# A wait for landing behind each two scatters of token rows in a fused attention and expert kernel

## The chip, the cores and the metric

The kernel runs on one core of one Trainium2 chip. The metric is the device time of one execution in microseconds (us), taken without the profiler; the median of three runs is given. A profile is one further execution of the same program, recorded by the hardware profiler.

## The reference, cut to what matters

```python
x = x + attention(rigid_transform(x, shift, angle))      # 2 x 1024 tokens of 256, 16 heads, causal
f = reaction_diffusion(x)                                # second differences along both axes
logits = f @ W_router + b_router                         # 8 experts
top_vals, top_idx = top_k(logits, 2)
w = softmax over the two chosen experts
for e in range(8):
    h = relu(f @ W1[e] + b1[e])                          # 256 -> 1024
    y = h @ W2[e] + b2[e]                                # 1024 -> 256
    out = out + y * w[:, e]                              # w is 0 where e was not chosen
x = x + out
```

Each of the 2048 tokens needs two experts only, so the kernel sorts tokens by expert and computes 39 tiles of 128 sorted rows.

## The kernel before, in words

One core does everything, with one instruction stream for each engine and semaphores between them. The order of the work is written out by hand.

**Stages.** First the image is sheared and interpolated, then attention runs in eight groups (four of heads for each of the two batches b = 0 and b = 1). Beside the last groups of b = 1 the router of b = 0 is computed. Then come the expert tiles. Nine of them (EARLY_TILES, tiles 0 to 8) hold rows of b = 0 alone, and the rest of b = 1 (its output projection, its reaction step, its router) is computed between them in a hand-written list (EARLY). The other 30 tiles are a loop.

**Scatters.** When the router of a batch has set each token's place (DVE, lines 1940 to 1966), GpSimd (POOL) writes the token rows to a sorted table `pairs_x` in HBM: function scatter (line 1010), one indirect DMA for 128 rows of 1032 bytes at line 1016, for each of the batch's 8 blocks and each of the two choices k. That is 16 scatters for a batch. All count on one semaphore, `scattered`, 16 for each.
- Batch 0: 16 scatters in a row, while attention of b = 1 ends on TensorE (PE) and ScalarE (ACT).
- Batch 1: between the expert tiles. Blocks go two by two (4 scatters); behind the second two stands add_tile(2), behind the fourth two add_tile(3).

**An expert tile t.** SyncE (SP) loads its rows (line 733, x_tile, from `pairs_x`), its W1 (line 720) and its W2 (line 726), 1 MB each, three tiles deep. PE turns the rows (turn_x, line 1478), makes the first product (line 1487), turns the hidden rows (line 1494) and makes the second product (line 1503). DVE copies the hidden rows out (line 2050) and in y_out adds the bias and scales (lines 2066, 2070), which signals `y_ready`. ACT applies the relu (line 1229). POOL adds the tile's result to HBM in add_tile (line 1020, an accumulating indirect DMA at line 1026).

**What ties them.** SP's row loads of tiles 0 to 2 wait for all 16 scatters of batch 0 (line 748), and four weight loads stand behind them in SP's queue. The row load of tile 9 waits for all 32. PE runs in order, so everything behind turn_x(0) waits for the rows of tile 0. y_out(t) waits until add_tile(t - 3) has landed, since there are three y_tile buffers: `dve.wait_ge(y_stored, (t - (SLOTS - 1)) * 16)`. The second product of tile t waits until y_out(t - 1) has read the bank. add_tile(t) waits for y_out(t) and for add_tile(t - 1) to land. POOL runs in order too: add_tile(2) and (3) stand behind the scatters ahead of them.

pool_hold (line 771) is a wait of POOL followed by an increment of a semaphore that nothing waits for.

Of the kernel before, what the change touches and what calls it, by code (L numbers as in the profile page):

```python
# [179 lines left out]
def build(nc, x, shift, angle, zx, zy, zr, wq, bq, wk, bk, wv, bv, wo, bo, wr, br, w1, b1, w2, b2, consts, out):  # L180
    ctx = ExitStack()
    with ctx:
# [3 lines left out]
        def sem(name):  # L186
            return ctx.enter_context(nc.semaphore(name))
# [256 lines left out]
        scattered = sem("scattered")  # L444
# [55 lines left out]
        def attention_plan():  # L500
# [19 lines left out]
            for n in range(2 * NG):  # L520
# [16 lines left out]
                if n == NG + 3:  # L537
# [16 lines left out]
                 ("first", 8, 0), ("second", 7, 0), ("h", 8, 0), ("second", 8, 0)]  # L554
        LIST_BEHIND, LAST_BEHIND = ("second", 3), ("first", 6)
        assert sum(k for _, _, k in EARLY) == len(LAST_PLAN)
        BEHIND, at_ = {}, 0
        for what_, t_, k_ in EARLY:
# [212 lines left out]
        def pool_hold(semaphore, value):  # L771


            nc.gpsimd.wait_ge(semaphore, value)
            nc.gpsimd.sem_inc(pool_held, 1)
# [61 lines left out]
        def _(pool):  # L837
# [172 lines left out]
            def scatter(b, blocks):  # L1010

                pool.wait_ge(slots_ready, b + 1)
                pool.wait_ge(weighed, b + 1)
                for i in blocks:
                    for k in range(2):
                        g_.indirect_dma_start(pairs_x.rearrange("r d -> (r d)").unsqueeze(0),  # L1016
                                              bass.IndirectOffsetOnAxis(ap=x_index[:, k, i:i + 1], axis=1),
                                              du_rows[:, i, 2 - 2 * k:ROW - 2 * k], None).then_inc(scattered, 16)

            def add_tile(t):  # L1020
                pool_hold(y_ready, t + 2)
                if t:
                    pool_hold(y_stored, 16 * t)
                if t == FIRST_LAST:
                    pool_hold(copied, 16)
                g_.indirect_dma_start(results if t < FIRST_LAST else out.rearrange("b s d -> (b s) d"),  # L1026
                                      bass.IndirectOffsetOnAxis(ap=home[:, t:t + 1], axis=0), y_tile[t % SLOTS],
                                      None, compute_op=ALU.add).then_inc(y_stored, 16)
# [4 lines left out]
            for n in range(NG + 2, 2 * NG):  # L1033
                group_of_v(n)
            pool.wait_ge(pairs_cleared, 16 * (NG + 1))
            scatter(0, range(SB))
            sideways(1)
            pool.wait_ge(base_stored, 16)
            for t in range(2):
                add_tile(t)  # L1040
            for k in range(SB // 2):
                scatter(1, range(SB + 2 * k, SB + 2 * k + 2))
                if k % 2:
                    add_tile(2 + k // 2)
# [496 lines left out]
        def _(dve):  # L1541
# [367 lines left out]
            def choose(b):  # L1909

                own = slice(b * SB, (b + 1) * SB)
                iota = const("experts").unsqueeze(1).broadcast_to([P, SB, E])
                lg_, cand_, idx_ = lg[:, own], cand[:, own], route[:, 6, own]

                def wide(a):
                    return a.unsqueeze(2).broadcast_to([P, SB, E])

                for turn, hot in enumerate((hot_1[:, own], hot_2[:, own])):
                    m = route[:, 2 + turn, own]
                    steps.do(v.reduce_max(m, lg_, AX_X))  # L1920
                    tt(cand_, lg_, wide(m), ALU.is_equal)
                    stt(cand_, iota, float(-E), cand_, ALU.add, ALU.mult)
                    steps.do(v.tensor_reduce(idx_, cand_, AX_X, ALU.min))
                    ts(idx_, idx_, float(E), ALU.add)
                    tt(hot, iota, wide(idx_), ALU.is_equal)
                    if turn == 0:
                        stt(lg_, hot, -3.0e38, lg_, ALU.mult, ALU.add)
                tt(both[:, own], hot_1[:, own], hot_2[:, own], ALU.add)
                dve.sem_inc(chosen_ready, 1)
                gap, _, m1, m2 = (route[:, i, own] for i in range(4))  # L1930
                tt(gap, m2, m1, ALU.subtract)
                dve.sem_inc(gap_ready, 1)
# [200 lines left out]
```

## Time and profile before

| what | value |
|---|---|
| median of 3 runs without the profiler | 964.36 us (960.53 to 966.77) |
| span of the profiled execution, first to last instruction | 990.0 us |
| time of the profiled execution itself | the page gives its span alone |
| PE busy | 732.5 us, 74% of the span |
| DVE, ACT, POOL busy | 52%, 36%, 31% |
| chain that ended last, largest shares | PE 55%, DVE 17%, DMA 10% |
| the same chain, "another core or an unknown queue" | 3% |

The median is 25.6 us below the profiled span. POOL's rows for an indirect DMA show the time in which the engine writes descriptors; the transfer itself comes later and is seen in the rows of queue q0 (software_dynamic). q1 (hardware_dynamic) carries the loads that SP issues. A wait marked "remote" and the chain's "another core or an unknown queue" mean that the profile shows no instruction whose end lies near the end of the wait.

### The profile page before, as it was taken

The page shows a single profiled execution, that of the slowest core. Times are in us where ns is not written, and L with a number is a line of the kernel's source. Part 1 is how long each engine was busy: PE and PEld are TensorE (multiplying, and loading weights), DVE is VectorE, ACT ScalarE, POOL GpSimd, SP SyncE. Part 2 cuts the span into 40 slices and gives each one's busy share as a digit, 9 for nine tenths or more (in the row PEclk, how much of TensorE's full clock was granted, in tenths as well). Part 3 has the DMA queues.
Part 4 walks back from the last instruction along what each step waited for, and adds up shares of the span by engine and source line. Part 5 has one row for each costly group of instructions (what it writes and reads, how often), then busy time and mean ns, then how long its engine had stood idle before and what let it go on. Part 6 is the DMA issues. An engine that isn't in the chain of part 4 may idle for free.

```text
span 990.0 us, 13623 instructions
## 1 busy us (share of the span) xinstructions
PE 732.5 (74%) x4035; PEld 437.9 (44%) x4035; DVE 515.9 (52%) x1052; ACT 360.4 (36%) x912; POOL 310.5 (31%) x292
## 2 busy tenths in 40 slices
PE   0440122835878889888999949997779999999993
PEld 0430111421333434433455413774557777666663
DVE  6446555777557664767777732654323333333331
ACT  0222333361566635363654535210212222222220
POOL 1114454876789623001100061107211111122121
PEclk9875555867899999999999979998899999999997
DMA  6998887896753017979310043957669999899961
GB/s 212 311 272 312 293 305 248 307 292 218 225 180 140 3 65 245 334 232 353 111 45 1 2 129 119 302 187 223 202 214 309 295 293 302 287 374 297 296 183 16
DMA packets 136206, 216.13 MB, mean 218 GB/s; under 512 B 10357, under 2 KB 102058, under 8 KB 135978
## 3 DMA queue, kind: packets, MB, share of 16 engines
q1 hardware_dynamic: 114808, 150.78, 46.5%
q0 software_dynamic: 16784, 61.51, 19.8%
q10 hardware_dynamic: 4546, 3.08, 1.1%
q8 instruction: 25, 0.41, 0.2%
q14 instruction: 43, 0.35, 0.1%
HBM read 160.87 MB, written 56.37 MB: 219 GB/s over the span
## 4 chain that ended last, share of the span: by engine, by line
PE 55%; DVE 17%; DMA 10%; issue 6%; ACT 4%; another core or an unknown queue 3%; POOL 2%; SPq 1%; ACTq 0%; POOLq 0%; DVEq 0%
PE psum L1503 13%; PE psum L1487 13%; DVE arena L1734 7%; PE psum L1428 6%; PE psum L1257 5%; PE psum L1442 5%; PE psum L1494 3%; DMA arena<-table,tap_col 3%; DMA arena<-qk_rows 2%; DMA table<-arena 2%; ACT arena L1180 2%; PE psum L1391 1%; POOL arena L881 1%; PE psum L1270 1%
## 5 line engine op out<-in xcount | busy, mean ns | idle before, releaser
L1180 ACT ACTIVATE arena<-psum 128x512 f32<-128x512 f32 (+3 forms) x384 | 171.2, 492 | 151.8 <-PE psum L1447 95.5
L1734 DVE TENSOR_REDUCE arena<-psum 128x2 f32<-128x1024 f32 (+2 forms) x192 | 176.2, 955 | 68.7 <-PE psum L1263 47.2
L1229 ACT ACTIVATE arena<-psum,b_cols 128x128 f32<-128x128 f32 x312 | 84.7, 382 | 269.9 <-PE psum L1494 248.0
L1503 PE MATMUL psum<-arena 128*128 128x256 f32 x624 | 147.2, 391 | 12.7 <-ACT arena L1229 12.7
L1487 PE MATMUL psum<-arena 128*128 128x512 f32 x312 | 142.8, 601 | 1.9 <-issue 1.8
L1442 PE MATMUL psum<-arena 99*128 99x512 bf16 (+3 forms) x384 | 115.9, 340 | 28.8 <-ACT arena L1180 23.0
L1503 PEld LDWEIGHTS psum<-arena 128*128 128x128 f32 x624 | 119.8, 197 | 30.1 <-issue 14.2
L1257 PE MATMUL psum<-arena 96*128 96x512 bf16 (+3 forms) x384 | 107.8, 347 | 33.6 <-DMA arena<-qk_rows 17.5
L2050 DVE COPY arena<-psum 128x1024 f32<-128x1024 f32 x39 | 47.8, 1225 | 93.7 <-PE psum L1487 92.4
L1428 PE MATMUL psum<-arena 128*32 128x512 f32 (+3 forms) x768 | 86.1, 521 | 0.5 <-ACT arena L1180 0.5
L1026 POOL DMA_INDIRECT results<-arena,home x23 | 36.4, 1581 | 156.0 <-DVE arena L2070 105.9
L1487 PEld LDWEIGHTS psum<-arena 128*128 128x128 f32 x312 | 57.1, 193 | 59.9 <-issue 59.9
L2066 DVE TENSOR_TENSOR arena<-psum,arena 128x256 f32<-128x256 f32 x39 | 16.6, 425 | 126.9 <-PE psum L1503 93.6
L1257 PEld LDWEIGHTS psum<-arena 96*128 96x128 bf16 x384 | 35.3, 102 | 104.4 <-DVE arena L1734 52.1
L1442 PEld LDWEIGHTS psum<-arena 99*128 99x128 bf16 x384 | 37.9, 100 | 80.1 <-ACT arena L1180 50.6
L1307 PE MATMUL psum<-cst,arena 128*128 128x128 f32 x16 | 5.5, 447 | 89.5 <-DVE arena L1773 89.5
L1298 PE MATMUL psum<-cst,arena 128*128 128x128 f32 (+1 forms) x180 | 33.9, 372 | 49.8 <-DMA arena<-padded,band_col 47.6
L1026 POOL DMA_INDIRECT result<-arena,home x16 | 24.8, 1552 | 103.6 <-DMA result<-arena,home 61.9
L1447 PE MATMUL psum<-mask_kq,ident_b 128*128 128x128 bf16 x256 | 54.9, 224 | 0.0
L1263 PE MATMUL psum<-mask_qk,ident_b 128*128 128x128 bf16 x256 | 54.1, 230 | 0.0
L1298 PEld LDWEIGHTS psum<-cst,arena 128*128 128x128 f32 (+1 forms) x180 | 30.9, 190 | 52.2 <-issue 36.1
L1016 POOL DMA_INDIRECT pairs_x<-warped_words,x_index x32 | 31.0, 969 | 66.8 <-DVEq L1944 57.7
(215 smaller groups left out, 985.2 us busy)
## 6 DMA issues: line engine op xcount, KB each, us to landing
arena<-L_ffn_W SPq DMA_DIRECT2D x78, 1024.0 KB, 5.4
pairs_x<-zeros SPq DMA_DIRECT2D x4, 4160.0 KB, 25.8
arena<-qk_rows SPq DMA_DIRECT2D x16, 768.0 KB, 7.2
table<-arena SPq DMA_DIRECT2D x20, 384.0 KB
qk_rows<-arena SPq DMA_DIRECT2D x16, 384.0 KB, 6.2
arena<-pairs_x SPq DMA_DIRECT2D x39, 130.0 KB, 4.6
qk_rows<-arena SPq DMA_DIRECT2D x16, 256.0 KB, 6.3
padded<-arena SPq DMA_DIRECT2D x2, 1328.0 KB
```

The lines of the kernel that those rows point to most:

```text
L1026: g_.indirect_dma_start(results if t < FIRST_LAST else out.rearrange("b s d -> (b s) d"), bass.IndirectOffsetOnAxis(ap=home[:, t:t + 1], a ...
L1180: nc.scalar.activation(probs[at % 2][h][:, q0:512], banks[turn % SCORE_BANKS][:, q0:512], ACT.Exp, scale=DH ** -0.5).then_inc(exp_done, 1)
L1229: ins = nc.scalar.activation(hidden_t[:, f], banks[3 + f // 4][:, (f % 4) * P:(f % 4 + 1) * P], ACT.Relu, bias=b1_cols[:, bass.ds(e, 1), f])
L1257: ins = t_.matmul(bank[:, 0:keys], stacks[0:KROWS, bass.ds(g, 1), 0, head, qb * P:(qb + 1) * P].squeeze(1).squeeze(1), stacks[0:KROWS, bas ...
L1263: ins = t_.matmul(bank[:, at_:at_ + P], ident_b[:], mask_qk[:], start=False, stop=True)
L1298: ins = t_.transpose(banks[g][0:w, r * P:(r + 1) * P], band[u][:, at_:at_ + w], ident)
L1428: ins = t_.matmul(banks[OUT_BANK][32 * h:32 * h + 32, q0:512], v_group[:, n % 2, kt, h], probs[at % 2][h][:, q0:512], start=first, stop=last)
L1442: ins = t_.matmul(bank[:, q0 - half * 512:512], stacks[0:KROWS + 3, g, 1, h, kt * P:(kt + 1) * P], stacks[0:KROWS + 3, g, 0, h, q0:(half + ...
L1447: ins = t_.matmul(bank[:, at_:at_ + P], ident_b[:], mask_kq[:], start=False, stop=True)
L1487: ins = t_.matmul(banks[half], x_t[:, c], w1_slot[u][:, c, half * 512:(half + 1) * 512], start=c == 0, stop=c == DC - 1)
L1503: ins = t_.matmul(banks[5][:, 0:D], hidden_t[:, f], w2_slot[u][:, f], start=f == 0, stop=f == FC - 1)
L1734: return v.reduce_max(part[:, 2 * pair:2 * pair + 2, qb], psum[:, first:first + 2, 0:keys], AX_X)
```

## The change

Behind the two scatters of each block, POOL waits until all scatters so far have landed.

```diff
@@ -1016,6 +1016,7 @@
                         g_.indirect_dma_start(pairs_x.rearrange("r d -> (r d)").unsqueeze(0),
                                               bass.IndirectOffsetOnAxis(ap=x_index[:, k, i:i + 1], axis=1),
                                               du_rows[:, i, 2 - 2 * k:ROW - 2 * k], None).then_inc(scattered, 16)
+                    pool_hold(scattered, 16 * 2 * (i + 1))
 
             def add_tile(t):
                 pool_hold(y_ready, t + 2)
```

POOL's instructions for batch 0, before: the first scatter waits for the router's places, and the other 15 follow it.

```order
L1016 DMA pairs_x<-warped_words,x_index 1x4293120 [waits weighed,slots_ready,pairs_cleared]
L1016 DMA pairs_x<-warped_words,x_index 1x4293120 x15
L831 TENSOR_TENSOR arena<-x 128x2x254 [waits reacted,x1_ready]
L832 TENSOR_SCALAR arena<-x 128x2
L833 TENSOR_SCALAR arena<-x 128x2
```

The same place on POOL in the changed kernel (its first pairs; the pattern repeats up to the eighth).

```order
L1016 DMA pairs_x<-warped_words,x_index 1x4293120 [waits weighed,slots_ready,pairs_cleared]
L1016 DMA pairs_x<-warped_words,x_index 1x4293120
L1016 DMA pairs_x<-warped_words,x_index 1x4293120 [waits scattered]
L1016 DMA pairs_x<-warped_words,x_index 1x4293120
L1016 DMA pairs_x<-warped_words,x_index 1x4293120 [waits scattered]
L1016 DMA pairs_x<-warped_words,x_index 1x4293120
```

Nothing changes places; every second scatter now carries a wait for `scattered`.

POOL's instructions for batch 1, before: the blocks of four scatters, with add_tile(2) and add_tile(3) (L1026) between and behind them.

```order
L1016 DMA pairs_x<-warped_words,x_index 1x4293120 [waits weighed,slots_ready]
L1016 DMA pairs_x<-warped_words,x_index 1x4293120 x3
L1016 DMA pairs_x<-warped_words,x_index 1x4293120 [waits weighed,slots_ready]
L1016 DMA pairs_x<-warped_words,x_index 1x4293120 x3
L1026 DMA results<-arena,home 2176x256 [waits y_ready,y_stored]
```

The same place on POOL in the changed kernel, where the line of add_tile's DMA is L1027.

```order
L1016 DMA pairs_x<-warped_words,x_index 1x4293120 [waits weighed,slots_ready]
L1016 DMA pairs_x<-warped_words,x_index 1x4293120
L1016 DMA pairs_x<-warped_words,x_index 1x4293120 [waits scattered]
L1016 DMA pairs_x<-warped_words,x_index 1x4293120
L1016 DMA pairs_x<-warped_words,x_index 1x4293120 [waits scattered,weighed,slots_ready]
L1016 DMA pairs_x<-warped_words,x_index 1x4293120
L1016 DMA pairs_x<-warped_words,x_index 1x4293120 [waits scattered]
L1016 DMA pairs_x<-warped_words,x_index 1x4293120
L1027 DMA results<-arena,home 2176x256 [waits scattered,y_ready,y_stored]
```

Four such waits now stand ahead of add_tile(2), the last on its own instruction, and four more ahead of add_tile(3). The other engines' instructions are the same in both kernels.

## Rows read from the trace of the kernel before

**Rows 1.** Chain that ended last, 570 to 600 us: start us, us, what.
```profile
576.94 4.68 another core or an unknown queue
...
584.67 8.28 another core or an unknown queue
```
**Rows 2.** The same view, 670 to 725 us.
```profile
674.78 21.24 another core or an unknown queue
```
**Rows 3.** Timeline, 674 to 712 us: start us, us, engine, line, operation [idle before <- releaser].
```profile
675.34 3.62 PE L1503 MATMUL psum<-arena 128*128 128x256 f32 x16
...
684.48 1.97 PE L1494 MATMUL psum<-cst,arena 128*128 128x128 f32 x8 [5.52 <-issue]
686.24 5.76 PE L1487 MATMUL psum<-arena 128*128 128x512 f32 x8
694.59 0.42 DVE L2066 TENSOR_TENSOR arena<-psum,arena 128x256 f32<-128x256 f32 x1 [9.64 <-remote]
696.68 2.17 ACT L1229 ACTIVATE arena<-psum,b_cols 128x128 f32<-128x128 f32 x8 [21.89 <-remote]
698.95 6.30 PE L1503 MATMUL psum<-arena 128*128 128x256 f32 x16 [6.73 <-ACT arena L1229]
705.09 1.04 PE L1494 MATMUL psum<-cst,arena 128*128 128x128 f32 x8
705.96 3.60 PE L1487 MATMUL psum<-arena 128*128 128x512 f32 x8
```
**Rows 4.** Waits of SP's queue: total us, times, longest us.
```profile
SPq L715 <- remote: 16.5, 1, 16.5
```
**Rows 5.** Timeline of POOL, 560 to 800 us.
```profile
572.91 1.06 POOL L1016 DMA_INDIRECT pairs_x<-warped_words,x_index  x1 [42.33 <-DVEq L1944]
574.27 0.99 POOL L1016 DMA_INDIRECT pairs_x<-warped_words,x_index  x1 [0.30 <-issue]
...
592.10 0.96 POOL L1016 DMA_INDIRECT pairs_x<-warped_words,x_index  x1 [0.30 <-issue]
653.23 1.61 POOL L1026 DMA_INDIRECT results<-arena,home  x1 [13.31 <-DVE arena L2070]
670.20 0.99 POOL L1016 DMA_INDIRECT pairs_x<-warped_words,x_index  x1 [15.36 <-DVEq L1944]
692.41 1.61 POOL L1026 DMA_INDIRECT results<-arena,home  x1 [0.30 <-issue]
697.48 1.59 POOL L1026 DMA_INDIRECT results<-arena,home  x1 [3.46 <-issue]
716.67 1.55 POOL L1026 DMA_INDIRECT results<-arena,home  x1 [7.41 <-DMA results<-arena,home]
723.97 1.55 POOL L1026 DMA_INDIRECT results<-arena,home  x1 [5.76 <-issue]
```
**Rows 6.** DMA queues, 594 to 595 us: packets, MB, share of 16 engines.
```profile
q0 software_dynamic: 15, 0.00, 0.8%
```
**Rows 7.** Timelines: SP's row load, DVE's scaling, PE at tile 0 and tile 7.
```profile
595.74 2.40 SPq L733 DMA_DIRECT2D arena<-pairs_x  x3
612.38 0.44 PE L1478 MATMUL psum<-cst,arena 128*128 128x128 f32 x2
651.98 0.36 DVE L2070 TENSOR_SCALAR arena<-arena,weight 128x256 f32<-128x256 f32 x1
717.38 3.62 PE L1503 MATMUL psum<-arena 128*128 128x256 f32 x16
```
**Rows 8.** DMA issues, 560 to 610 us: KB each, us to landing.
```profile
arena<-pairs_x SPq DMA_DIRECT2D x3, 130.0 KB, 2.0
```
**Rows 9.** Busy time by stretch: A:B us, PE, PEld, DVE, ACT, POOL, PEclk, DMA share, GB/s.
```profile
684.00:690.00 6.00, 5.52 (x13) 3.43 (x14) 0.95 (x4) 0.00 (x0) 4.48 (x6) 0.50 0.38 128
```
**Rows 10.** DMA queues, 581 to 584 us.
```profile
q1 hardware_dynamic: 179, 0.73, 86.4%
```

## The prediction

> **What bounds the kernel now.** I read the chain that ended last first, because PE is busy 74% of the span and the question is what the rest is. In the two stretches where POOL scatters, the chain has its only large pieces of "another core or an unknown queue": 4.68 and 8.28 us in batch 0 [rows 1] and 21.24 us in batch 1 [rows 2]. Next the timeline, to see who waits there. In batch 1 DVE's L2066 waits 9.64 us and ACT's L1229 21.89 us for something "remote" [rows 3], and SP's queue waits 16.5 us in the same way [rows 4]. By the code, DVE and SP wait for the second product of tile 4 and ACT for the turned hidden rows of tile 5. Their PE rows end at 675.34 + 3.62 = 678.96 and at 684.48 + 1.97 = 686.45 [rows 3], some 16 and 10 us before the waits end. So PE had done the work, by its rows, and its signals reached three engines late, while POOL was issuing scatters. I call this the held signals. In batch 0 it is ACT that waits, also for PE.
>
> What they cost the profiled execution, from the chain: batch 0, 4.68 + 8.28 = 13.0 us, all in attention's last group. Batch 1: PE finished first product and turned rows at 686.24 + 5.76 + 0.2 = 692.2 and could start the second product of tile 5 only at 698.95, 6.7 us; that product then took 6.30 us instead of 3.62 (PE had stood still), another 2.7. Together 22.4 us. The rest of the 21.24 us is covered by PE's own work and by DVE's list of tiles, which PE waits for (5.52 us) either way.
>
> The decisive number is another: the runs without the profiler take 964.36 us, 25.6 us less than the profiled span of 990.0. If the held signals belong to the profiled execution only, the sum closes to 3.2 us (990.0 - 22.4 = 967.6). I know of no other 22 us that a recorder could add to a kernel whose PE rows have the same durations tile after tile. So I take it as likelier that the timed runs have few or none of these stalls, and that the change has little to win there.
> The Trainium skill (NOTIFIC, the notification-queue block, section 7.1) says that the block which writes the profiler's records can push back on the engines that produce them, though it was never seen to overflow. That would be such a cause; the trace cannot tell it from a real hold on the signals.
>
> **The change part by part.** It adds 16 waits on POOL and moves nothing. Each pair of scatters now costs its own round trip. Within a pair: second scatter starts 574.27 - 572.91 = 1.3 us after the first [rows 5]. Landing: the last scatter of batch 0 starts at 592.10, and the last packets of q0, empty ones, fall in 594 to 595 [rows 5, 6], so 2.0 us after its start. Restart of POOL after a wait: DVE's L2070 ends at 651.98 + 0.36 = 652.34 and the add starts at 653.23, 0.9 us [rows 5, 7]. A pair's period is 1.3 + 2.0 + 0.9 = 4.2 us, against 2.6 before. From below: the restart costs no more than the 0.30 us between scatters, 3.6. From above: SP's row load, released by the last scatter, is issued at 595.74, 3.64 us after that scatter's start [rows 5, 7]; 1.3 + 3.6 = 4.9.
>
> Term C, rows of tile 0 come late. Batch 0 starts at 572.9 as before. The eighth pair starts at 572.9 + 7 x 4.2 = 602.3, plus 0.5 for the pair in flight while SP's first W1 load has the engines: from 581 to 584 there is no q0 packet, though POOL issued three scatters around it [rows 10]. It lands at 602.8 + 3.3 = 606.1, not 594.1. SP needs 1.6 us from landing to issue (594.1 to 595.74) and the rows 2.0 more [rows 7, 8]: 609.7. PE reaches turn_x(0) at 612.38 in the profile [rows 7] and at 612.4 - 13.0 = 599.4 without held signals. There it waits, in order, with everything behind it: +10.3 us. With a period of 3.6 it is +6, with 4.9 +15. In the profiled execution alone the wait would have hidden behind the stall (609.7 is before 612.4): this is where a gain of 13 us turns into one of 2.7.
> The Trainium skill (DMA: Bandwidth & Descriptors, "Queues, rings and completion order") says that each DMA engine goes round between its queues packet by packet. By that rule the pair in flight would share with the W1 load and the 0.5 us would be 0, and the waits of batch 1 would be close to the unloaded 4.2. The trace does not agree in 581 to 584, where q1 has 179 packets and q0 none.
>
> Term D, the clock. PE stands still some 10 us ahead of turn_x(0). After such a pause the granted clock is 0.50, the 1.2 GHz level, for about 6 us [rows 9], and the rows show what it costs: L1494 1.97 instead of 1.04 and L1487 5.76 instead of 3.60 [rows 3]; 3.1 us. Bounds 0 and 5.
>
> Term E, the adds behind the scatters of batch 1. Queued behind POOL's waits stand add_tile(2) and (3), and y_out(6) waits for add_tile(3) to land, second product 7 for y_out(6). With a period p from 670.2 [rows 5]: four pairs, add_tile(2) with 1.9 us of POOL, four pairs, add_tile(3), its landing 4.2 us later (692.41 to 697.48 less the restart), y_out: second product 7 can start at 670.2 + 8p + 7.0. Unloaded (p = 4.2) that is 710.8. But the weight loads run beside it, and adds that wait for their landing come 723.97 - 716.67 = 7.3 us apart there, against 5.1 at 692 to 697 when SP was stuck [rows 5]; 2 us more each. So p lies between 4.2 and 6.2; when PE stalls, the loads stop and p falls back, and I take 5.2: 718.8. Without held signals that product would start at 717.38 - 9.4 = 708.0 [rows 7]. +10.8 us, bounds 3 and 19. add_tile(4) follows 5 us behind and holds nothing more, and the row load of tile 9 is needed later.
>
> Sum of costs: 10.3 + 3.1 + 10.8 = 24.2 us. On the profiled execution: 990.0 - 22.4 + 24.2 = 991.8 us, so its span hardly moves. On the timed runs, without anything to win: 964.4 + 24.2 = 988.6 us. Every term's row comes from the one profiled execution; the median is taken as the base because I hold its stalls for absent.
>
> **The rivals.**
> Rival 1, the held signals are real and in the timed runs too, and pairs dissolve them. For it: three engines truly waited in the trace, and only beside scatters. Against it: then 25.6 us between span and median have no source. Time: 964.4 - 22.4 + 24.2 = 966.2, within 1%.
> Rival 2, the same, and the round trips are cheap, so that it ends faster. One mechanism: PE's signals flow during the scatters, and landing is quick enough not to take the place of the stall. It decides at costs under 12.8 us (22.4 - 9.6). With the low ends, C 6, D 1, E 3: 964.4 - 12.4 = 952.0. For it: add_tile(2) and (3) would only just be late at p = 3.6 to 4.2. Against it: the loads beside batch 1, and PE's start on tile 0, which is bound to the last landing in every case.
> Rival 3, the change doesn't do what it says: POOL's waits cost nothing that anyone waits for, 964 us. It would take landings that keep up with issue; the 2.0 us of rows 5 and 6 speak against it.
> Rival 4, held signals stay with two scatters in flight as with sixteen: PE's signals were still prompt behind the first four scatters of batch 0 (the first hole starts at 576.94, 4 us after the first scatter), so pairs with pauses should be too short for it. If they stay, the cost terms stand alone and the time is the forecast's.
>
> **How the numbers follow.** Forecast (with rival 4) 0.60, own range 974 to 1004 (the terms' low ends 6 + 0 + 3 and high ends 15 + 5 + 19). Rival 1 0.25, 957 to 981. Rival 2 0.08. Rival 3 0.07. About 1%, 9.6 us, is what a measurement of this kernel can tell from no change. Faster by more: rival 2 and a corner of rival 1, 0.10. Slower by more: nearly all of the forecast and a part of rival 1, 0.64. Within: 0.26. The range 957 to 1001 leaves out rival 2 and the forecast's upper tail.
>
> **What would show each step.** In the changed kernel's profile: scatters in twos, 4.2 us from pair to pair in batch 0; no "unknown queue" piece in the chain over 2 us beside them; the row load of tile 0 issued near 607.7 and PE's L1478 near 609.7, with the clock at 0.50 behind it; an L2066 of tile 6 that waits for the landing of an add near 718; a span near 992. I am wrong if the profile's span falls by 15 us or more (the costs were too high), and wrong about the base if the span stays near 990 while the median stays near 964: then the timed runs had the stalls.

## The result, and the profile after

The changed kernel takes 1008.83 us (median of 4 runs, 1006.52 to 1013.25), the kernel before 965.57 us (median of 4 runs, 960.53 to 967.66). The ratio is 1.0453, 95% interval 1.0411 to 1.0495: slower by 43.3 us. The forecast was 988.6 with a range to 1001; the direction was right and the size was not. The profiled execution took 1006.52 us by itself, with a span of 1004.3, so what the recorder sees and what the clock outside sees are 2.2 us apart. A few executions ran in a slower state (1102.42 us in one of the last kernel of the table below), which the ratios leave out and the medians do not; over the others alone the medians of "before, small loads" and "before, four adds moved" are 964.1 and 964.7.

The chain of the changed kernel in batch 0 (start us, us, what) answers to [rows 1].

```profile
577.26 5.91 DMA pairs_x<-warped_words,x_index
583.21 0.77 issue
583.97 0.97 POOL pairs_x L1016
585.25 2.43 DMA pairs_x<-warped_words,x_index
...
588.49 0.97 POOL pairs_x L1016
...
607.93 2.75 DMA pairs_x<-warped_words,x_index
611.44 2.12 DMA arena<-pairs_x
614.30 3.71 PE psum L1381 x8
...
628.29 3.63 PE psum L1488 x8
```

No piece of "unknown queue" is left. In its place the chain runs through every pair: 1.27 us between its two scatters, 2.43 to 2.75 us landing, 0.77 us until POOL starts the next, some 4.5 in all. One pair took 5.91 us to land. The same view in batch 1 answers to [rows 2].

```profile
676.66 6.92 DMA pairs_x<-warped_words,x_index
...
685.66 6.47 DMA pairs_x<-warped_words,x_index
...
694.26 2.43 DMA pairs_x<-warped_words,x_index
...
698.77 6.29 DMA pairs_x<-warped_words,x_index
706.03 1.61 POOL results L1027
...
722.94 2.58 DMA pairs_x<-warped_words,x_index
726.49 3.78 DMA results<-arena,home
732.07 6.58 PE psum L1504 x16
```

Three of the first four pairs needed 6.3 to 6.9 us to land (the third 2.43), and the pairs behind add_tile(2) 2.4 to 2.6. The second product of tile 7 (PE L1504, L1503 before) starts at 732.07, behind the landing of add_tile(3). The timeline shows SP's loads, and who waits for the late pieces.

```profile
577.00 0.42 SPq L720 DMA_DIRECT2D arena<-L_ffn_W  x1
611.44 2.58 SPq L733 DMA_DIRECT2D arena<-pairs_x  x3
613.61 0.69 PE L1479 MATMUL psum<-cst,arena 128*128 128x128 f32 x2 [18.59 <-DMA arena<-pairs_x]
675.37 0.99 POOL L1016 DMA_INDIRECT pairs_x<-warped_words,x_index  x1 [15.34 <-DVEq L1945]
676.36 0.38 SPq L726 DMA_DIRECT2D arena<-L_ffn_W  x1
685.25 12.48 SPq L726 DMA_DIRECT2D arena<-L_ffn_W  x2
698.61 0.38 SPq L720 DMA_DIRECT2D arena<-L_ffn_W  x1
710.65 0.42 DVE L2067 TENSOR_TENSOR arena<-psum,arena 128x256 f32<-128x256 f32 x1 [13.20 <-DMA results<-arena,home]
711.61 6.58 PE L1504 MATMUL psum<-arena 128*128 128x256 f32 x16 [10.37 <-DVE arena L2071]
726.25 1.47 SPq L733 DMA_DIRECT2D arena<-pairs_x  x2
731.11 0.42 DVE L2067 TENSOR_TENSOR arena<-psum,arena 128x256 f32<-128x256 f32 x1 [17.99 <-DMA results<-arena,home]
732.07 6.58 PE L1504 MATMUL psum<-arena 128*128 128x256 f32 x16 [9.57 <-DVE arena L2071]
```

These answer to [rows 3, 5, 7]: nothing waits for "remote" any more. Each slow pair has a 1 MB weight load issued beside it (577.00, 676.36, 685.25, and for the fourth pair of batch 1 the second load of the row at 685.25, issued near 697.4, and the one at 698.61). PE waits 18.59 us for the rows of tile 0, and 10.37 and 9.57 us for products 6 and 7.

### The profile page after: what moved, and what is told of

The parts are those of the page before. It is cut to its first block, busy times and chain, and to the rows that moved or that the text cites. A ratio compares the mean times of both kernels' runs of the same rounds, so it can differ in the third digit from the quotient of the medians.

```text
span 1004.3 us, 13639 instructions
## 1 busy us (share of the span) xinstructions
PE 732.9 (73%) x4035; PEld 440.9 (44%) x4035; DVE 515.1 (51%) x1052; ACT 359.8 (36%) x912; POOL 312.2 (31%) x292
## 4 chain that ended last, share of the span: by engine, by line
PE 49%; DVE 18%; DMA 16%; issue 7%; POOL 4%; ACT 3%; SPq 1%; POOLq 0%; DVEq 0%; ACTq 0%
PE psum L1504 12%; PE psum L1488 12%; DVE arena L1735 7%; DMA pairs_x<-warped_words,x_index 6%; PE psum L1429 5%; PE psum L1258 5%; PE psum L1443 4%; DMA arena<-table,tap_col 3%; PE psum L1495 3%; DMA table<-arena 3%; DMA arena<-qk_rows 2%; POOL arena L881 2%; POOL pairs_x L1016 2%; PE psum L1392 1%; PE psum L1271 1%
## 5 line engine op out<-in xcount | busy, mean ns | idle before, releaser
L1504 PE MATMUL psum<-arena 128*128 128x256 f32 x624 | 147.2, 391 | 25.9 <-DVE arena L2071 19.9
L1504 PEld LDWEIGHTS psum<-arena 128*128 128x128 f32 x624 | 119.7, 197 | 43.5 <-issue 27.7
L1443 PE MATMUL psum<-arena 99*128 99x512 bf16 (+3 forms) x384 | 113.8, 334 | 15.7 <-ACT arena L1181 9.9
L2051 DVE COPY arena<-psum 128x1024 f32<-128x1024 f32 x39 | 47.8, 1225 | 94.1 <-PE psum L1488 93.8
L1429 PE MATMUL psum<-arena 128*32 128x512 f32 (+3 forms) x768 | 83.0, 504 | 0.5 <-ACT arena L1181 0.5
L1027 POOL DMA_INDIRECT results<-arena,home x23 | 36.4, 1581 | 146.6 <-DVE arena L2071 57.6
L1299 PE MATMUL psum<-cst,arena 128*128 128x128 f32 (+1 forms) x180 | 36.2, 390 | 49.5 <-DMA arena<-padded,band_col 47.6
L1443 PEld LDWEIGHTS psum<-arena 99*128 99x128 bf16 x384 | 37.5, 99 | 64.3 <-ACT arena L1181 37.8
L1027 POOL DMA_INDIRECT result<-arena,home x16 | 25.0, 1560 | 101.5 <-DMA result<-arena,home 57.3
L1299 PEld LDWEIGHTS psum<-cst,arena 128*128 128x128 f32 (+1 forms) x180 | 33.0, 200 | 51.8 <-issue 36.2
## 6 DMA issues: line engine op xcount, KB each, us to landing
pairs_x<-zeros SPq DMA_DIRECT2D x4, 4160.0 KB, 25.6
arena<-qk_rows SPq DMA_DIRECT2D x16, 768.0 KB, 11.4
```

Of the source, the lines that this page charges most:

```text
L1299: ins = t_.transpose(banks[g][0:w, r * P:(r + 1) * P], band[u][:, at_:at_ + w], ident)
L1429: ins = t_.matmul(banks[OUT_BANK][32 * h:32 * h + 32, q0:512], v_group[:, n % 2, kt, h], probs[at % 2][h][:, q0:512], start=first, stop=last)
L1443: ins = t_.matmul(bank[:, q0 - half * 512:512], stacks[0:KROWS + 3, g, 1, h, kt * P:(kt + 1) * P], stacks[0:KROWS + 3, g, 0, h, q0:(half + ...
L1504: ins = t_.matmul(banks[5][:, 0:D], hidden_t[:, f], w2_slot[u][:, f], start=f == 0, stop=f == FC - 1)
```

## The experiments

Four distances, all read from the timelines, put the runs side by side: from the first scatter of batch 0 to SP's load of the first rows (a), from the first scatter of batch 0 to that of batch 1 (b), from there to SP's load of tile 9's rows, which waits for all 32 scatters (c), and from there to the end of the span (d). The profiled kernel ahead of the prediction had 22.8, 97.3, 38.3 and 281.5. Where the text below gives a run's distance from the kernel before, it is from the 966.2 us of the first row.

| kernel | median us | ratio to before, 95% interval | a | b | c | d |
|---|---|---|---|---|---|---|
| before, again | 966.2 | 0.999 (0.995 to 1.002) | 22.6 | 85.9 | 25.0 | 281.2 |
| the change | 1008.8 | 1.045 (1.041 to 1.050) | 40.4 | 104.3 | 50.9 | 278.1 |
| batch 0 alone | 983.8 | 1.019 (1.013 to 1.026) | 40.6 | 105.2 | 25.0 | 283.2 |
| batch 1 alone | 991.9 | 1.026 (1.021 to 1.032) | 22.7 | 87.7 | 51.8 | 281.3 |
| one pair behind | 978.4 | 1.011 (1.006 to 1.017) | 26.8 | 90.7 | 36.9 | 278.0 |
| behind each four | 989.1 | 1.024 (1.020 to 1.028) | 29.3 | 93.7 | 39.3 | 282.4 |
| W1 behind the rows | 1010.7 | 1.046 (1.041 to 1.050) | 37.7 | 105.0 | 50.3 | 282.4 |
| small loads | 1000.3 | 1.038 (1.032 to 1.043) | 41.1 | 105.6 | 41.3 | 278.1 |
| before, small loads | 964.8 | 0.998 (0.994 to 1.002) | 22.7 | 85.9 | 24.8 | 280.2 |
| two adds moved | 1006.9 | 1.042 (1.038 to 1.046) | 40.8 | 106.3 | 51.5 | 276.1 |
| before, two adds moved | 965.4 | 0.999 (0.997 to 1.001) | 22.6 | 84.3 | 25.5 | 279.5 |
| four adds moved | 997.5 | 1.035 (1.029 to 1.041) | 40.6 | 104.4 | 54.5 | 263.5 |
| before, four adds moved | 966.3 | 1.002 (0.999 to 1.005) | 22.5 | 84.2 | 34.1 | 269.5 |

### The kernel before, profiled again

No edit.

> The kernel before, unchanged, for a profile of a usual execution. If the held signals belong to the rare execution that was profiled first: a span near 963 us, no 'unknown queue' piece above 2 us in the chain beside the scatters, PE at tile 0's rows (L1478) about 26.5 us behind the first scatter of batch 0 and the second product of tile 7 about 38 us behind the first scatter of batch 1. If they are in every execution: a span near 990 us and those pieces again.

Ten runs, 959.43 to 970.65, one of them profiled: span 966.1, its own time 968.07. The chain has no piece of unknown queue, and the scatters run one into the next until SP loads the rows.

```profile
590.67 0.97 POOL pairs_x L1016
591.94 0.97 POOL pairs_x L1016
593.22 2.63 DMA pairs_x<-warped_words,x_index
596.61 2.08 DMA arena<-pairs_x
...
599.17 1.92 PE psum L1380 x8
...
602.14 4.67 PE psum L1487 x8
...
611.12 5.33 PE psum L1487 x8
```

And from its timeline:

```profile
598.74 0.44 PE L1478 MATMUL psum<-cst,arena 128*128 128x128 f32 x2 [0.76 <-DMA arena<-pairs_x]
659.92 0.99 POOL L1016 DMA_INDIRECT pairs_x<-warped_words,x_index  x1 [15.36 <-DVEq L1944]
693.98 3.62 PE L1503 MATMUL psum<-arena 128*128 128x256 f32 x16
```

Two things follow. The held signals belong to the one execution profiled first: b and c were 11.4 and 13.3 us longer in it, 24.7 together, where the prediction had put them at 22.4. And PE reached the first rows 598.74 - 574.01 = 24.7 us behind the first scatter, after a wait of 0.76 us, so the rows of tile 0 were already just on the path: no slack at all. Both distances that the prediction had worked out by subtraction are shorter: 24.7 us where 26.5 was expected, and 693.98 - 659.92 = 34.1 us to the second product of tile 7 where 38 was expected.

### The hold in one batch alone

```diff
-                    pool_hold(scattered, 16 * 2 * (i + 1))
+                    if b == 0:
+                        pool_hold(scattered, 16 * 2 * (i + 1))
```

> The waits in batch 0 alone. Theory (round trips in series; each batch has its own path to the end): terms C and D as the changed kernel's trace has them, 16 + 4 = 20 us, so 985 us. Rival (the batches share one path, so that a shift ahead of the expert tiles is taken up by slack later, and batch 1 makes the whole cost): within 5 us of the kernel before, 970 us or less. PE at tile 0's rows 42 to 43 us behind the first scatter in either case.

The other run has `if b == 1:` in that place.

> The waits in batch 1 alone. Theory: term E as the changed kernel's trace has it, 19 to 23 us, so 985 to 989 us, and together with the run for batch 0 the 43 us of the change. Rival (shared path): 1000 us or more. y_out of tiles 5 and 6 wait for an add to land, over 10 us each.

Measured: 983.84 us with batch 0's holds and 991.87 with batch 1's, 17.6 and 25.6 us above 966.2. The first is within 2 us of the 985 expected, the second just above the 985 to 989 expected, and both rivals (970 or less, 1000 or more) fall. The sum, 43.2, is the change's 43.3: the halves add up and neither covers for the other. In the table batch 0's holds lengthen a and b and leave c; batch 1's lengthen c alone. Both are well above the terms of the prediction (13.4 for C and D, 10.8 for E).

### Waiting for the pair before the last

```diff
-                    pool_hold(scattered, 16 * 2 * (i + 1))
+                    if i:
+                        pool_hold(scattered[(i - 1) % 2], 32 * ((i - 1) // 2 + 1))
```

with two semaphores, counted in turn by block.

> As many waits as the change, but each for the pair before the last (two semaphores, one for even and one for odd blocks), so that two pairs can be in flight. Theory (the cost is the round trip in series): without load the pair before has landed when the wait is reached (2.6 us of issue against 2.4 of landing), the period falls to 2.6 to 2.9 us in batch 0, and beside weight loads some waiting stays: 966 to 976 us. Rival (each wait of POOL costs by itself, by its restart, whatever it waits for): a period near 3.5 to 4.5 us in batch 0 and 985 to 1005 us.

Measured 978.44 us, just above the 966 to 976 expected, 12 above before and 30 below the change: most of the cost is POOL standing through each landing, and it goes when the wait looks one pair back. The timeline of POOL shows the part that stays.

```profile
581.08 0.96 POOL L1018 DMA_INDIRECT pairs_x<-warped_words,x_index  x1 [0.30 <-DMA pairs_x<-warped_words,x_index]
...
588.61 0.97 POOL L1018 DMA_INDIRECT pairs_x<-warped_words,x_index  x1 [4.03 <-DMA pairs_x<-warped_words,x_index]
...
675.18 0.96 POOL L1018 DMA_INDIRECT pairs_x<-warped_words,x_index  x1 [5.09 <-DMA pairs_x<-warped_words,x_index]
```

Between most pairs POOL waits no longer than the 0.30 us it always has. It stands 4.03 us at 588.61, behind a W1 load issued at 580.99, and in batch 1 5.09 at 675.18 and again 4.77 and 3.76 us at 684.71 and 695.16. That was more than expected, and it pointed to the weight loads.

### Holding behind each four scatters

```diff
-                    pool_hold(scattered, 16 * 2 * (i + 1))
+                    if i % 2:
+                        pool_hold(scattered, 16 * 2 * (i + 1))
```

> The change with the hold behind every second block only: GpSimd waits behind each four scatters, so eight holds instead of sixteen. Theory, each hold costs its own round trip (2.4 us landing and 0.8 until the next scatter starts, less the 1.3 us... of one scatter's spacing: 2.0 us of 4.5 in place of 2.5) and a hold that meets a weight load about 3.5 to 4.3 us more: batch 0 three restarts fewer costs 6 + 3.5 + 3 for the cold clock = 12 to 13 instead of 17.6; batch 1, with three of its four holds meeting a load, 10 to 15 instead of 25. Together 988 to 994. Rival, the cost is in meeting the loads and not in the number of waits: then batch 0 costs nearly what it did, and the time stays above 998. Rival, the cost goes by the number of waits alone: half of 43, 988 or less.

989.06 us, inside the first theory's interval, but only just above what "by the number of waits alone" gave, so the time does not tell these two apart. The distances do in part: in batch 0, where here no wait met a load (each ended 2.4 to 2.9 us behind the last scatter's start), a is 6.7 us above before (22.6 to 29.3), as three restarts at 2.0 say; c rose by 14.3, with two of its landings above 6 us.

### W1's load behind the row loads

```diff
-            load_w1(0)
             sp.wait_ge(scattered, 16 * NBLK)
             for t in range(SLOTS):
                 load_x(t)
+            load_w1(0)
```

> The change with the load of the first expert's W1 issued behind the first three row loads instead of among batch 0's scatters. Theory: a pair of scatters in flight gets little or nothing from the DMA engines while a weight load runs, so the second pair's 8.0 us (5.9 us landing) come from that load, and all pairs of batch 0 now take 4.5 us; the first rows are loaded 3.5 us earlier behind the first scatter (about 37 us instead of 40.4). In time: 3.5 us less at most, 1005.3, and nothing if W1, now loaded some 6 us ahead of the first product, lands too late. Rival: the long second pair belongs to the start of the scatters and not to the load; then it stays at 8 us, and the time at 1009 or above.

The second pair's landing is the first in this piece of chain, and the next bound is the second.

```profile
579.28 2.48 DMA pairs_x<-warped_words,x_index
...
614.06 5.65 DMA arena<-L_ffn_W
619.75 6.77 PE psum L1488 x8
```

With the load gone the pair lands in 2.48 us instead of 5.91 and all pairs of batch 0 take 4.5 to 5.0 us: the load, not the start of the scatters, held it. The rows are loaded 2.7 us earlier (a 37.7, where about 37 was expected). But the time did not fall, 1010.7 (1005.51 to 1014.52): W1 now lands at 619.7 and the first product starts at 619.75, 46.8 us behind the first scatter; in the change it started at 618.85, 47.8 behind. What is gained on the rows goes into W1 and a slower start of PE (its first product takes 6.77 us instead of 4.91). The expected 3.5 us were a ceiling, and the case "W1 too late" came.

### Small weight loads beside batch 1's scatters

```diff
-                sp.dma_start(w1_slot[t % SLOTS], w1[bass.ds(expert_of(t), 1)].squeeze(0)
-                             .rearrange("(c p) f -> p c f", p=P)).then_inc(w1_in[t % SLOTS], 16)
+                wide = P if t in (8, 9) else FC * P
+                sp.dma_start(w1_slot[t % SLOTS][:, :, 0:wide], w1[bass.ds(expert_of(t), 1)].squeeze(0)
+                             .rearrange("(c p) f -> p c f", p=P)[:, :, 0:wide]).then_inc(w1_in[t % SLOTS], 16)
```

and W2 likewise, cut to `[:, 0:1]` of its eight parts for t in (6, 7, 8). Both kernels of this section leave out the rest of these weights, so they measure time only.

> The change with five weight loads that fall among batch 1's scatters cut to an eighth (W2 of tiles 6, 7, 8 and W1 of tiles 8, 9: 128 KB instead of 1 MB each; the rest of those weights is left out, so the output of these tiles differs). Theory, a pair in flight gets nothing from the DMA engines while a 1 MB weight load runs: in the changed kernel four of batch 1's eight pairs take 6.3 to 7 us to land (periods 8.6 to 9.0) and each has such a load issued in it; with small loads all eight land in 2.4 to 2.8 us, and from the first scatter of batch 1 to SP's load of tile 9's rows it takes 37 to 41 us instead of 50.9. In time 995 to 999. Rival, the long landings come from the adds or from the place of the rows written, not from the loads: four pairs stay above 5 us and the time within 4 us of 1008.8.

And the control:

> The control of the run ahead of it: the kernel before, without holds, with the same five loads cut to an eighth. Its sixteen scatters run without a wait at 1.27 us each, so the loads cost them nothing; only adds and products that met a load can gain. Theory: 960 to 967, so that the change beside its small loads costs 30 to 34 us instead of 43. Rival, small loads help everything behind them alike: then this run gains as much as the other, and is at 955 or below.

DMA issues of batch 1 in the small-loads kernel, 675 to 717 us (count, KB each, median us from issue to landing):

```profile
arena<-L_ffn_W SPq DMA_DIRECT2D x5, 128.0 KB, 2.3
pairs_x<-warped_words,x_index POOLq DMA_INDIRECT x16, 2.6
```

The same in the run with batch 1's holds and whole loads, 657 to 690 us:

```profile
arena<-L_ffn_W SPq DMA_DIRECT2D x5, 1024.0 KB, 6.6
pairs_x<-warped_words,x_index POOLq DMA_INDIRECT x9, 4.2
```

With five loads cut to an eighth, c falls from 50.9 to 41.3, where 37 to 41 was expected, and no pair of batch 1 takes over 3.9 us to land. The time is 1000.33, 8.5 below the change (997.47 to 1003.30; 995 to 999 was expected, a narrow miss). The control is unmoved at 964.83, so the gain is the holds' own. Beside small loads the change costs 1000.3 - 964.8 = 35.5 us, a little above the 30 to 34 expected. (The expectation spoke of four slow pairs in batch 1; the profile shown above has three.) So about 8 of the 43 us are batch 1's pairs standing behind weight loads. The other 35 stay with no large load beside batch 1's scatters. That they are the round trips themselves is what the run one pair behind says, which gives 30 of the 43 back with all loads in place; batch 0's one pair behind W1 is among the 35, and freeing that gained nothing.

### Moving adds ahead of batch 1's scatters

```diff
-            for t in range(2):
+            for t in range(3):
                 add_tile(t)
             for k in range(SB // 2):
                 scatter(1, range(SB + 2 * k, SB + 2 * k + 2))
-                if k % 2:
-                    add_tile(2 + k // 2)
+                if k == 0:
+                    add_tile(3)
```

> The change with two adds moved on GpSimd: the add of tile 2 goes ahead of batch 1's scatters, the add of tile 3 behind the first four of them (in the change they stand behind the first eight and behind all sixteen). Theory A, the cost of the second batch comes through the buffers of the products: in the changed kernel's profile second product 6 waits for the add of tile 2 (issued 706.03) and product 7 for the add of tile 3 (726.49). With both early, products 6 and 7 wait for nothing, and the next that can wait is product 8, for the add of tile 4, which still stands behind all sixteen scatters (near 722, landing near 726). Product 8 stood at 742.48 and would stand near 728 to 730: 12 to 15 us less, 993 to 997. If adds 2 and 3 were the whole of the second batch's cost it would fall to what the hold in batch 0 alone costs, 984. Rival B, the length of the scatters itself sets the time, through the rows of tile 9 that SP loads behind them (726.25): then within 4 us of the change, 1005 to 1009.

1006.89 us. By the time alone rival B has it. The profile says otherwise.

```profile
702.62 3.62 PE L1504 MATMUL psum<-arena 128*128 128x256 f32 x16
710.38 3.62 PE L1504 MATMUL psum<-arena 128*128 128x256 f32 x16
736.64 6.56 PE L1504 MATMUL psum<-arena 128*128 128x256 f32 x16 [21.77 <-DVE arena L2071]
...
746.86 6.57 PE L1488 MATMUL psum<-arena 128*128 128x512 f32 x8 [3.44 <-issue]
```

Products 6 and 7 wait for nothing, as theory A had it, and the whole wait reappears in one piece, 21.77 us, ahead of product 8, which needs add_tile(4) from behind all sixteen scatters. A chain of adds with three buffers was unblocked at two links and stood at the third. Then DVE's y_out for tile 8 waits 8.87 us for add_tile(5), which lands late beside the loads that SP had held back. DVE's copy of tile 9's turned rows stands behind that y_out (it starts at 746.36), and so PE's first product of tile 9 starts at 746.86.

With four adds moved (tile 2 ahead, tiles 3, 4 and 5 behind four, eight and twelve scatters):

```diff
-                if k == 0:
-                    add_tile(3)
-            for t in range(4, EARLY_TILES):
+                if k < 3:
+                    add_tile(3 + k)
+            for t in range(6, EARLY_TILES):
```

> The change with four adds among or ahead of batch 1's scatters: tile 2 ahead of them, tiles 3, 4 and 5 behind four, eight and twelve. With two moved adds (1006.9) the wait went to product 8, which stood 21.8 us for the add of tile 4 behind all sixteen scatters. Theory A, only the adds' place couples the scatters to the products: product 8 then runs near 720, some 16 us earlier, the next thing behind the scatters is SP's load of tile 9's rows near 735, which turn and first product of tile 9 use; 993 to 999. Rival B, the end of batch 1's scatters sets the time whatever is moved on GpSimd (in all eight traces so far the span ends 276 to 283 us behind SP's load of tile 9's rows): 1004 to 1010.

997.47 us (991.60 to 1001.12), inside theory A's interval; rival B falls. The span now ends 263.5 us behind SP's load of tile 9's rows where all kernels up to this one had 276 to 283. By itself that says little: the load also comes 3.6 us later (c 54.5), since adds now stand among the scatters, and in the kernel before with the same moves, below, d falls by 11.7 us with the time unchanged. What counts is c and d together, which fall by 11. PE's timeline:

```profile
705.19 3.62 PE L1504 MATMUL psum<-arena 128*128 128x256 f32 x16
712.62 5.38 PE L1504 MATMUL psum<-arena 128*128 128x256 f32 x16 [2.94 <-ACT arena L1230]
728.10 0.69 PE L1479 MATMUL psum<-cst,arena 128*128 128x128 f32 x2 [10.10 <-DMA arena<-pairs_x]
729.36 5.95 PE L1488 MATMUL psum<-arena 128*128 128x512 f32 x8 [0.56 <-issue]
```

Product 8 starts at 712.62 and does not wait for an add. The wait is now 10.10 us for the rows of tile 9, which SP may load only when all scatters have landed. So the adds carried some 11 us of batch 1's cost (1008.8 - 997.5), and behind them stood a second bound, the rows.

### The same moves without holds

Both moves in the kernel before, as candidates to beat it.

> The kernel before, without holds, with the same two adds moved: tile 2 ahead of batch 1's scatters, tile 3 behind the first four. If the adds behind sixteen unheld scatters already hold the products a little (in the profile of the kernel before run again, second product 5 comes 12.9 us behind product 4 where its neighbours take 8.2 to 8.5, and the add of tile 2 is issued 17 us after its product), 960 to 964 against 966.2. Rival: what delays product 5 is the batch's other work on TensorE and VectorE, and the adds cost nothing in the kernel before: 965 to 968. Slower than 970 only if batch 1's scatters, which start about 2 us later, set something: rows of tile 9 are loaded 684.9 and used behind 705, so this has some 20 us of slack.

> The kernel before, without holds, with the same four adds moved; the candidate to beat both. With two moved adds it stood at 965.4, and product 8 still waited 2.95 us for ScalarE and 1.8 to 2.9 us followed ahead of tile 9's first product. If these come from the adds of tiles 4 and 5, which land 6 to 7 us apart behind the scatters, 960 to 963. If adds behind sixteen scatters at 1.27 us have slack enough, 964 to 967. Above 968 only if the later end of the scatters (some 3 to 5 us) is late for tile 9's rows.

965.41 and 966.26 us, no difference from 966 in either. Behind sixteen scatters at 1.27 us apart the adds have slack enough. The 2.95 us that product 8 waits for ScalarE in the kernel before are still there in both, so they did not come from adds. With four adds moved the rows of tile 9 are loaded 9.1 us later (c 34.1) and no one waits for them. No version tried beats the kernel before.

## Why the prediction was right in direction and short in size

**The base was right.** "The timed runs have few or none of these stalls" holds: the second profile has none, its span is 2 us below its own time, and its 966.1 stands beside the 967.6 that the subtraction of 22.4 us gave. That was the step that turned a seeming gain into a loss. Rivals 1, 2 and 4 needed the held signals in the usual execution and fall with them; rival 3 falls by the 43 us. The reverse has to be said too: that the profile of the change shows no held signals proves nothing for pairs, since the kernel before shows none either in its usual execution.

**Term C, the rows of tile 0, failed in size: 10.3 us forecast, 17.8 measured.** PE's first turn_x stands 613.61 - 571.05 = 42.6 us behind the first scatter, 24.7 before. Three steps of the working were off. The period of an undisturbed pair was put at 4.2 us and is 4.54: the landing was read as 2.0 from packets (2.43 to 2.75 by the semaphore), the restart as 0.9 (0.77). With the first pair's 4.94 that is 2.4 us over six periods. The pair beside the W1 load was charged 0.5 us and takes 7.98 instead of 4.54: 3.3 more than charged. And PE without stalls was put at 26.5 us behind the first scatter, 1.8 too late. The third part shows a habit worth dropping: a stall was subtracted from one execution and the rest taken as exact, although removing a stall also removes what it had pushed back.

**Term D, the clock, 3.1 forecast, 0.6 measured.** From the first turn_x to batch 1's first scatter the change takes 675.37 - 613.61 = 61.76 us, the kernel before 659.92 - 598.74 = 61.18. The slow rows are there after the long pause (granted clock 0.50 from 613.6 to 618.0; L1381 3.71 where before had 1.92), but the kernel before has slow rows of its own a little later (0.51 from 601 to 604), in its first product (4.67, the change 4.91) and its second one (5.33, where the change has 3.63). The cost of a clock level was counted as if the other kernel had none.

**Term E, the adds behind the scatters, 10.8 forecast, 22.6 measured.** The mechanism was right: product 7 waits for add_tile(3), at 732.07, and the formula 8p + 7.0 gives 56.2 us behind the first scatter with the measured p against 56.7 read. The step that failed is the choice of p = 5.2. Measured, (726.49 - 675.37 - 1.92) / 8 = 6.15 us, nearly the upper bound of 6.2: three pairs take 8.5 to 9.0 and five 4.5 to 4.8, since a load in the way costs a pair some 4 us and not 2. That is 8 x 0.95 = 7.6 us. The reason given for 5.2, "when PE stalls, the loads stop and p falls back", is not what happened. The third pair is quick because SP issues no load from 685.7 to 697.4, and the kernel before profiled again has a like gap (670.2 to 682.4). From the fifth pair on it is SP itself that stands: its queue waits for all 32 scatters ahead of tile 9's rows, with every later load behind. SP's waits, 670 to 730 us (total us, times, longest us):

```profile
SPq L732 <- DMA pairs_x<-warped_words,x_index: 26.5, 1, 26.5
```

That tile 9's row load waits for all scatters was known; that it holds back the weight loads too was not drawn from it. Another 3.7 us of the difference in term E are the base of product 7, put 37.8 us behind the first scatter and found at 34.1 in the kernel before profiled again. "The row load of tile 9 is needed later" was true only as long as the adds were later still: with the adds moved it is the next bound.

**The sum.** 17.8 + 0.6 + 22.6 = 41.0 us up to the start of product 7, 24.2 forecast; counted from the first scatter to the ends of the two spans it is 41.2. That these agree so well is partly luck. Product 7 itself then takes 6.58 us instead of 3.62, at a granted clock of 0.50 from 732 to 736, so product 8 is 25.6 us late and not 22.6, and 2.9 us are regained behind it. The forecast had counted the clock for tile 0 alone. That the medians are 43.3 us apart and the two spans 38.2 is the spread of the work ahead of the first scatter (571.05 against 574.01) and of single executions. The forecast's own range ended at 1004 and the range given ended at 1001, its width spent below, on rival 1; the measured 1008.8 is above both. Terms C and E both came out above their own high ends (15 and 19): they share one cause, how long a pair takes, and share the too late base, so their errors added.

## What to carry to other kernels

A wait for landing behind each small indirect DMA costs its whole round trip each time: here 4.5 us a pair where issue alone takes 2.5, and 8.0 to 9.0 when a 1 MB load runs beside it; if a limit on what is in flight is wanted, wait for the pair before the last one, which gave back 30 of the 43 us here. Price a wait by the landing seen from the waiting engine, not by the packets, and look up which large load is issued among its transfers, and what would stop those loads. Before relying on a stall of a profile, look whether the span agrees with the time of that same execution or of a second profile.

## What the hardware showed that was not expected

A scatter that POOL has issued can stand still for microseconds beside a weight load. In the changed kernel a pair was issued by 677.6 and landed at 683.6; a W2 load had been issued at 676.36. The DMA queues from 678 to 681 us:

```profile
q1 hardware_dynamic: 705, 0.72, 94.3%
```

705 packets of q1 and none of q0 in three microseconds, as in [rows 10]. It is the pair's second scatter that stands: of the pair's 96 packets 48 run from 676 to 678, beside the load's, and the other 48 only from 681 to 683.6. In the pair that starts at 583.97, with no load beside it, they run from 585.5 to 586.5 and from 586.5 to 587.7. The Trainium skill (DMA: Bandwidth & Descriptors, "Queues, rings and completion order") has each engine go round its queues packet by packet; by that the second scatter would have been served in these 3 us if its descriptors were ready, and the trace shows no packet of it. Whether they were ready, or were themselves late beside the load, no run here separates, so this does not show the page wrong.

Signals of PE that reach other engines 10 to 16 us late beside sixteen scatters issued without a wait [rows 3] were seen in one profiled execution of that kernel and not in the second one, nor as a time near 992 us in its ten runs. What sets them off stays open.
